# Eight landing places for the weight pieces, three products over zeros, and moved neighbour products in a decoder layer on one core

## The reference

```python
x = _layernorm(x + _L0_attn_ref(x, L0_attn_wq, L0_attn_wk, L0_attn_wv, L0_attn_wo), axis=-1)
x = _layernorm(x + _L0_xattn_ref(x, ctx_4096, L0_xattn_weight), axis=-1)
x = _layernorm(x + _L0_ffn_ref(x, L0_ffn_A, L0_ffn_B, L0_ffn_Wr, L0_ffn_br), axis=-1)
```

## Time and profile before

| what | value |
|---|---|
| time, median of 3 runs | 1413.91 us (1412.76 to 1415.48) |
| profiled execution: its own time / its span | 1418.97 us / 1417.2 us |
| PE busy | 1358.8 us, 96% of the span |
| DVE / ACT / POOL busy | 1095.7 / 931.8 / 985.4 us |
| granted TensorE clock, mean | 0.983 |
| HBM read / written | 131.83 MB / 34.47 MB |

### The profile page before, as it was taken

How to read it: one execution, slowest core, us unless ns; L and a number is a source line. 1 busy time by engine, 2 the same in 40 slices (tenths; PEclk the granted TensorE clock), 3 DMA queues, 4 the chain that set the end, 5 groups by cost and what they waited for, 6 DMA issues and landing times. The chain is left out here.

```text
span 1417.2 us, 32292 instructions
## 1 busy us (share of the span) xinstructions
PE 1358.8 (96%) x8288; PEld 1057.2 (75%) x8288; DVE 1095.7 (77%) x3868; ACT 931.8 (66%) x3258; POOL 985.4 (70%) x937
## 2 busy tenths in 40 slices
PE   6899999999999999999986899999999999999995
PEld 4677777777777777777763788888888888888873
DVE  5777877878787777878875588777888777887774
ACT  5778878888787887888884455545555455555443
POOL 3776777777777776777773777667777677776763
PEclk9999999999999999999997999999999999999997
DMA  7435445354453544445467766666566676667651
GB/s 245 111 106 159 135 128 158 115 161 125 137 157 115 163 116 146 150 119 158 131 202 215 172 165 160 161 174 155 159 164 155 166 169 149 164 159 162 158 119 45
DMA packets 108862, 213.04 MB, mean 150 GB/s; under 512 B 26640, under 2 KB 32272, under 8 KB 108816
## 3 DMA queue, kind: packets, MB, share of 16 engines
q1 hardware_dynamic: 108624, 212.25, 54.4%
q10 hardware_dynamic: 192, 0.26, 0.1%
HBM read 131.83 MB, written 34.47 MB: 117 GB/s over the span
## 5 line engine op out<-in xcount | busy, mean ns | idle before, releaser
L459 PE MATMUL wo_ps<-weights,halves 128*128 128x512 f32 x2304 | 571.6, 399 | 10.5 <-DVE weights L637 10.3
L459 PEld LDWEIGHTS wo_ps<-weights,halves 128*128 128x128 f32 x2304 | 421.6, 189 | 146.8 <-issue 59.1
L718 ACT ACTIVATE pexp<-sm,smin 128x128 f32<-128x128 f32 x1024 | 397.9, 391 | 102.0 <-DVE smin L590 98.1
L1074 PE MATMUL wo_ps<-weights,halves 128*128 128x512 f32 x1488 | 401.3, 402 | 2.0 <-DVE yz L1177 2.0
L1427 POOL TENSOR_TENSOR prods<-prod,prods 128x512 fp32r<-128x512 f32 x192 | 260.2, 1363 | 133.1 <-ACT prods L1321 128.1
L847 POOL TENSOR_TENSOR pn<-pexp,prec 128x512 f32<-128x512 f32 x256 | 265.5, 1042 | 96.2 <-DVE prec L597 96.2
L1074 PEld LDWEIGHTS wo_ps<-weights,halves 128*128 128x128 f32 x1488 | 273.4, 190 | 61.1 <-issue 3.7
L590 DVE CUSTOM_DVE_ANT_0 sm<-s_ps,mask_t 128x128 f32<-128x128 f32 x1024 | 231.8, 282 | 26.5 <-PE s_ps L489 24.5
L1321 ACT CAST prods<-prod 128x512 fp32r<-128x512 f32 x192 | 118.8, 621 | 167.1 <-DVE prod L1211 124.0
L1211 DVE TENSOR_TENSOR prod<-att,x 128x512 f32<-128x512 f32 x192 | 186.8, 988 | 12.7 <-DMA att<-sim_scratch 10.2
L718 ACT ACTIVATION_READ_ACCUMULATOR pexp<-sm,smin 128x1 f32 x1024 | 192.5, 188 | 0.0
(11 more groups left out here) (96 smaller groups left out, 1684.0 us busy)
## 6 DMA issues: line engine op xcount, KB each, us to landing
att<-sim_scratch SPq DMA_DIRECT2D x192, 252.0 KB
pt<-blocks SPq DMA_DIRECT2D x636, 64.0 KB, 2.0
ctx_t<-in_ctx SPq DMA_DIRECT2D x32, 576.0 KB, 5.1
raw<-in_xT SPq DMA_DIRECT2D x32, 512.0 KB, 4.0
raw<-ot_scratch SPq DMA_DIRECT2D x32, 512.0 KB, 6.7
xn<-in_x SPq DMA_DIRECT2D x32, 512.0 KB, 7.5
out<-late SPq DMA_DIRECT2D x32, 512.0 KB, 6.1
ot_scratch<-ot SPq DMA_DIRECT2D x63, 256.0 KB, 2.1
```

Source lines behind the costliest of these rows:

```text
L459: mm = pe.matmul(qkv_ps[(par + g) % 2][:], xs[:, par, xl, k], w_sb[:, wl, g, k], start=(k == 0 and n == 0), stop=(k == KT - 1 and n == 2))
L718: ins = nc.scalar.activation(pexp[:, c % 2, i * P:(i + 1) * P], sm[:, c % 2, i * P:(i + 1) * P], ACT.Exp, bias=smin[:, c % 2, i:i + 1], sc ...
L1074: mm = pe.matmul(wo_ps[n][:], os_t[:, par, ol, k], wo_sb[:, wl, k, n * BANK:(n + 1) * BANK], start=(k == 0 and m == 0), stop=(k == KT - 1 ...
```

## The change

The weight pieces get eight landing places instead of four: the second four lie in `pt`. The memset of `pt` therefore moves behind piece 7 (POOL waits for `w_lo` 8), and POOL first clears `sm[:, 0]` (an eighth of the size of `pt`), over which PE then does three products (`WARM`) before the first projection. The neighbour products of batch 0 move on POOL from step 1 into step 0; those of batch 1 move from POOL to DVE (`neighbours_of_second`, one instruction of 128x1024); those of batch 2 move from p = 5 and 7 to p = 6 and 7, behind the scaling. SP issues x of batch 3 in step 1 instead of at the head of step 2.

```diff
-    STAGES = 4
+    STAGES = 8
+    WARM = 3
...
     def stage(n):
-        u, i = divmod(n % STAGES, NI // WK)
-        return blocks[:, u, i * 2:(i + 1) * 2].rearrange("p k j i q -> p k (j i q)")
+        u, i = divmod(n % 4, NI // WK)
+        home = (blocks, pt)[n % STAGES // 4]
+        return home[:, u, i * 2:(i + 1) * 2].rearrange("p k j i q -> p k (j i q)")
...
             if at_step(a, 0):
-                sp.wait_ge(set_up, 2)
+                sp.wait_ge(set_up, 3)
...
             if valid(t + 1):
-                if not at_step(t, 0) and not at_step(t, 1):
+                if not at_step(t, 0) and not at_step(t, 1) and not at_step(t, 2):
                     load_x(t + 1, 1 - par)
                 load_ctx(t + 1)
...
             if valid(a):
                 wait(sp, pv_done, after(a - 1, NU, 1))
+            if at_step(t, 1):
+                load_x(3, 1)
             if valid(t):
                 wait(sp, sq_done, after(t, 1, 1))
                 wait(sp, summed, after(t, 1, 1))
...
             if at_step(t, 0):
+                pe.wait_ge(set_up, 2)
+                for _ in range(WARM):
+                    pe.matmul(s_ps[0][:], sm[:, 0, 0:P], sm[:, 0], start=True, stop=True)
                 for s in range(SLOTS):
...
+        def neighbours_of_second():
+
+            dve.wait_ge(c_in, 16 * 2)
+            dve.wait_ge(summed, 1)
+            dve.tensor_tensor(nb[:], ctx_t[:, 0:D], ctx_t[:, S:S + D], ALU.mult).then_inc(nb_done, 2)
+
...
+                if at_step(t, 1) and p == 4:
+                    neighbours_of_second()
                 if valid(a):
                     mask_min(a, p)
...
         pool.memset(zero[:], 0.0).then_inc(set_up, 1)
-        pool.memset(pt[:], 0.0).then_inc(set_up, 1)
+        pool.memset(sm[:, 0], 0.0).then_inc(set_up, 1)
         low_x(0, 0, 0)
         low_x(0, 0, 1)
+        pool.wait_ge(w_lo, PIECES - STAGES + STAGES // 2)
+        pool.memset(pt[:], 0.0).then_inc(set_up, 1)
...
             if at_step(t, 0):
                 add_k(0, 0)
                 add_q(0, 0, 0)
+                neighbour(0, 0)
+                neighbour(0, 1)
                 return
...
-                if at_step(t, 1) and p == 0:
-                    neighbour(0, 0)
-                    neighbour(0, 1)
...
-                if at_step(t, 1) and p == 4:
-                    neighbour(1, 0)
-                    neighbour(1, 1)
-                if p in (5, 7) and valid(t + 1):
+                if at_step(t, 1) and p in (6, 7):
+                    neighbour(2, p - 6)
+                if p in (5, 7) and valid(t + 1) and not at_step(t, 1):
                     neighbour(t + 1, (p - 5) // 2)
```

More of the change, by code:

```diff
@@ L193, in part1 @@
     consts_in = sem("consts_in")
-    w_in = [sem(f"w_in{n}") for n in range(4)]
+    w_in = [sem(f"w_in{n}") for n in range(8)]
     w_hi = sem("w_hi")
```

## The result

The changed kernel takes 1410.72 us (median of 12 runs, 1408.13 to 1414.93) beside 1416.57 us for the kernel before (median of 12, 1412.76 to 1423.17): a ratio of 0.995, 95% interval 0.9936 to 0.9963. That is faster by 0.4 to 0.6%, or 5.2 to 9.1 us, where 7.6 were forecast. The kernel before took longer in these twelve runs than in the three of the prediction, so the ratio says more than the absolute time: 1410.72 itself lies 0.7 above the forecast range (1403.2 to 1410.0), while the ratio carried over to the 1413.91 of the prediction gives 1406.8, where 1406.3 was forecast. In the profiled executions the span went from 1417.2 to 1410.0 us.

The account below looks back on a forecast made before the run. PE was taken as the bound from batch 2's scores on, so only their shift from 80.73 us counts. The terms, -3.5 + 0 + 0 - 4.1 = -7.6, took the median of 1413.91 to 1406.3 us, range 1403.2 to 1410.0.

Parts of the forecast that it names:

- Term 1: Start up to batch 0's scores: eight landing places, limited by the moved memset, bring them from 35.10 to 31.6, -3.5 us.
- The memset beside DVE: At the start: POOL's memset of `pt` doesn't shut out DVE's subtractions; if it did, x ready about 2.1 us later.
- rival (a): At the start: memset excludes DVE, or pieces come slower with eight in flight; gain only 1.4 to 1.8, 1408.3 us; chance 0.13.
- Term 2: Before the first projection: products over zeros bring 0, up to 2.0 us without the wait for the sum of K.
- Term 3: Step 1: the moved neighbour products of batches 0 and 1 bring 0 us, bounds -0.4 and +1.2.
- Term 4: Step 2: earlier eighth exponents and x of batch 3 shorten PE's wait and keep the clock up, -4.1 us, bounds -1.05 and -4.7.
- Behind batch 2: Loop from batch 2's scores on: PE is the bound, 22.30 us per step, an earlier start reaches the end one to one.
- Rival (c): Ahead of the turn of K: the new 2.4 us wait lets the clock fall, 1.6 us come back, 1407.9; chance 0.06.
- Rival (e): Loop: ACT lags PE, the 0.35 wait for the copy of Q returns every step, 10.2 us, 1416.5; chance 0.03.

Follow-up runs that it names:

- places only: Kernel before with only the eight landing places and the moved memset of `pt`, no products over zeros; scores of batch 2 at 77.54 us instead of 80.73.

## Why the prediction was right

The mechanism held at each place, the sum to batch 2 was 7.6 and measured 7.1 in the first profile, and its parts erred both ways: Term 1 brought 1.6 less than forecast, Terms 3 and 4 together 1.1 more. That the spans too differ by 7.2 is in part luck, since the loop lost 2.4 us and the head of part 2 gained 2.3, and the change touches neither. In the changed kernel's second profile batch 2 is only 5.2 earlier.

**Term 1** (-3.5) was mis-sized: -1.9 in the first profile, -2.7, -2.4 and -2.0 in three others with the same POOL order, and -0.1 in the one where the clock fell. The path was as described (memset, sum, turn, 9.0 us to the scores: 24.14 to 33.16 is 9.02). Two of its figures were too small, by about 0.8 us each. Piece 7 was cast at 16.70, not 15.9: the first piece was 0.2 late, piece 4 another 0.5, which the even pace of 1.26 from four pieces could not show. And from that cast to the turn of K it was 7.44, not 6.7, because the sum for K stood behind DVE's third subtraction and not its second. That is no matter of late pieces. With places only, where piece 7 was cast at 15.99, as forecast, POOL and DVE show the same:

```profile
18.36 3.54 POOL L856 MEMSET pt<- 128x4096 f32 x1 [10.73 <-DVE weights L638]
21.86 1.43 POOL L836 TENSOR_TENSOR rot<-rot 128x256 f32<-128x256 f32 x1
...
19.21 3.49 DVE L638 TENSOR_TENSOR weights<-blocks,weights 128x1024 fp32r<-128x1024 f32 x3
```

The working let DVE's rotation and two subtractions end 3.7 us after piece 7's subtraction, 0.2 behind the memset. They took 3.2 (18.3 to about 21.5), so that DVE had begun a third when the memset ended at 21.9. The alternation of POOL and DVE was in the working; how far DVE would be by then was what it had wrong.

**The memset beside DVE**: none, as taken. The trace agrees with the rule of the Trainium skill that was cited (SBUF — State Buffer, Who interferes with whom): three subtractions in 3.49 us, the first two wholly beside a memset of 3.54. Of rival (a) the exclusion fell, and the slower pieces came, by less than its price.

**Term 2** (0) held. What the products are worth without the wait ahead of K, where up to 2.0 was the bound, no pair of runs shows; the estimate above is 0.6.

**Term 3** (0, bound -0.4) came out at its bound, -0.43: DVE's added product (1.18) mostly filled a stretch in which DVE had idled 0.88 for the second scores of step 1, so the masks behind it were hardly later, and the copy of Q no longer late. But that hangs on who goes first. In the profile without products over zeros DVE's product and POOL's scaling met like this:

```profile
42.00 2.09 DVE L631 TENSOR_TENSOR nb<-ctx_t 128x1024 f32<-128x1024 f32 x1
...
41.97 1.04 POOL L862 TENSOR_TENSOR pn<-pexp,prec 128x512 f32<-128x512 f32 x1
```

and in the changed kernel's:

```profile
42.45 1.18 DVE L631 TENSOR_TENSOR nb<-ctx_t 128x1024 f32<-128x1024 f32 x1
...
42.41 2.12 POOL L862 TENSOR_TENSOR pn<-pexp,prec 128x512 f32<-128x512 f32 x1
```

Either the scaling waits for the product or the product for the scaling. In three of the eleven profiles with this edit it was the product (2.09 or 2.10); PE then waited 0.4 for the copy of K ahead of the turn of Q, and step 1 took 19.66 or 19.67, no less than before. In the other eight it took 19.14 to 19.18. So Term 3 is -0.4 or +0.1.

**Term 4** (-4.1, bound -4.7) measured -4.74. Since DVE's product filled idle time, the eighth exponents started at 52.10, 54.0 in the old time, not 55.1, and the forecast 0.6 of remaining wait was not there:

```profile
52.10 0.40 ACT L733 ACTIVATE pexp<-sm,smin 128x128 f32<-128x128 f32 x1 [0.54 <-DVE smin L597]
```

The bound had it. That both parts are needed, the load of x and the products, was in the working and is what the runs of each alone show.

**Behind batch 2** the prediction had a shift that goes through one to one. It does, but the loop varies by 2.4 us of itself, and the head of part 2 by about as much: from its first matmul to the end 648.6 us before and 646.3 after, with the clock over the first 31.4 us of it at 0.80 and 0.89 though nothing there was changed. **Rival (c)**, the clock that falls in the new wait, had 6 in 100 and a price of 1.6; it was absent in the first profile and present in the second, at 1.3, one of five profiles with this order on POOL (waits of 0.89 to 2.71 ahead of the turn of K). With the landing of the pieces and of x it is one reason for which the gain can vary from run to run; how often it comes in unprofiled runs is not shown. **Rival (e)**, a loop with ACT lagging, is real as a wait but belongs to both kernels.

## What to carry over

When two streams must both be early for a third to go on, each edit alone shows little; here 1.0 and 0.5 us became 4.5. So try them together before dropping one. Where an input lands at a different time in each execution, measure from the landing: the 2.27 us of the memset are the same in every pair of profiles then, and a worth of the products that one pair seemed to show goes away. A clearing that must wait for a buffer belongs behind the next instruction that the critical engine waits for, not ahead of it. And a load issued at the head of a step may sit behind a queue of others: moved one step ahead, it took all of PE's waits out of a loop. The runs spread less as well with it and the memset moved; which of the two did that is not shown.

## What was not expected of the hardware

- The clock fell after waits of 2.06, 2.55, 2.65 and 2.71 us on PE (scores at 2.09, 1.58 to begin with, 2.09 and a granted 0.57), but not after 2.13, 2.21 and 2.30. Where it falls differs from execution to execution of one kernel.
- Products over zeros raise the clock as others do, but three of them ended so early that it had often fallen back: the 48 matmuls took 12.73 to 12.80 us in four profiles with a half clock early in them (waits of 2.36 to 2.76 us in between), 11.64 in one without (wait of 2.30), 13.4 to 13.5 in the three without products and with eight places. With five products, two profiles showed full clock from the first matmul on. (Without products the clock column reads 1.00 between 9 and 12 us, but the seven matmuls that it has in that window are as many as the changed kernel had at 0.55, so it doesn't tell the clock there.)
- A product of 128x1024 on DVE and a scaling of 128x512 on POOL that start within 0.04 us of each other go one after the other, and the order differs between executions (1.18 and 2.12 us, or 2.09 and 1.04).
- The same transfers at the start are served at 320 GB/s in one execution and 419 in another between 9 and 12 us, and move the landing of piece 7 by up to 1.7 us.
